# Layer 2 of a four-layer graph kernel: the exact copy of X in two pieces of the rounded four-byte format instead of three bf16 pieces, masks multiplied at full width, every second mask of negative edges made by ScalarE

## The chip, the cores and the metric

The kernel runs on one core of a Trainium2 chip. The metric is the device time of one execution in microseconds (us); lower is better. TensorE (PE in the rows) multiplies, VectorE (DVE), ScalarE (ACT) and GpSimd (POOL) work elementwise, and SyncE (SP) issues most transfers. All wait for one another through semaphores.

## The reference, cut to what matters

`adj` is a 4096 x 4096 float32 matrix with about 1.5% nonzero entries, `x` is 4096 x 64. Four graph layers follow each other, each with a residual and a normalisation. The change is in the second:

```python
node_support = jnp.concatenate([(A_node > 0).astype(h.dtype) @ h, (A_node < 0).astype(h.dtype) @ h], axis=1)
edge_output = gru_cell(node_support, h, w_ih_e, w_hh_e, b_ih_e, b_hh_e)
...
hw = h @ W
h_plus = (node_adj > 0).astype(hw.dtype) @ hw
h_minus = (node_adj < 0).astype(hw.dtype) @ hw
e_plus = jax.nn.leaky_relu(jnp.concatenate([h_plus, h_minus], axis=1) @ a, ALPHA)
...
att = jax.nn.softmax(att, axis=1)
return att * edge_adj @ hw
```

So layer 2 needs four sums over the neighbours of each node: h weighted with the positive and with the negated negative entries of the adjacency matrix (its diagonal taken out), and h summed over the places of the positive and of the negative entries, where the matrix is a 0/1 mask.

## The kernel before

**Layers.** Layer 1 (a polynomial in the matrix, three rounds over it) ends near 501 us of the trace. Layer 2 runs from 529 to 978 us, layer 3 (a product with a decaying weight made from one-byte codes) starts at once behind it, and layer 4 follows. The matrix doesn't fit on the chip, so each layer streams it from memory.

**Layer 2.** The columns are done in `NQ` = 4 quarters (`q`) of 1024. A quarter has `NS` = 8 slots (`s`) of four row blocks of 128, loaded by SyncE with one 2 MB transfer each into one of `RING` = 4 ring slots. A slot is done in two pairs of blocks, so a quarter has `PAIRS` = 16 pairs (`m`), 64 in all. For a pair:

- VectorE extends the chain of neighbour counts that layer 3 needs (L2093, two per pair), makes the masks `more` (L2117, L2122: entry > 0) and `less` (L2118, L2124: entry < 0) in bf16, and then cuts the entries in the ring at zero in place (L2127). That last step needs ScalarE to have read them, and it releases TensorE (`rect_ready`). In four of the sixteen pairs of each quarter VectorE also takes out the diagonal (L2106, L2110, L2113).
- ScalarE makes `negs` (L1453, Relu of the negated entries) and one-byte codes from the chain (L1440), and sends them to memory.
- TensorE multiplies. For each of the two blocks and each half of 512 columns stand there a float32 product of X with the cut entries and one with `negs` (L947, L948), then three products of the bf16 pieces of X with `more` and three with `less` (L953, L955). Every product has 64 output rows; the two of a line number pair take the two halves of the array side by side. The sums lie in banks 0 to 3.

`more`, `less` and `negs` have two places each, so work on pair m may write them as soon as TensorE is done with pair m - 2 (`pair_used`).

**Work between the pairs.** The four queues are written out by hand. While the pairs of quarter q run, the rest of layer 2 for quarter q - 1 and q - 2 is put between them at fixed m: copies of the four sums out of the banks (`copy_sums`, m = 0), `score` (m = 2), score and share arithmetic on VectorE (m = 3 and 5), `weigh_sums` (m = 8), `hidden` on TensorE with `read_hidden` on ScalarE (m = 10 and 11, three banks), the gates (m = 13 to 15 and again at m = 1 and 2 of the next quarter), the normalisation (m = 4, 6, 7) and the pieces of layer 3's operand. In the last quarter ScalarE makes the first two weights of layer 3 (`make_decays`, L1426) at m = 12 and 14. Behind the last pair stand `copy_sums(3)` and `score(3)` ahead of layer 3's first products (`decayed`, L983 and L996).

**Ahead of layer 2** `split` (L1910) and `split_act` (L1228) cut X into its three bf16 pieces, VectorE and ScalarE in turn.

## Time and profile before

| | us |
|---|---|
| median of 3 runs | 1562.92 |
| lowest and highest | 1557.15, 1565.25 |
| the profiled execution | 1558.08 |
| its span, first to last instruction | 1556.3 |
| TensorE busy in the span | 1370.9 (88%) |
| VectorE busy | 1228.1 (79%) |
| ScalarE busy | 922.3 (59%) |
| layer 2, first to last pair | 449 |

The profiled execution is 1.8 us longer than its span and lies 4.8 us below the median. Busy times are sums over instructions, and the products of TensorE overlap in its pipeline: two products that take the two halves of the array count once, and a product starts before the one ahead of it has ended. What a product costs is read from the distance between starts. PEclk is the granted clock of TensorE as a share of its full speed of 2.4 GHz.

### The profile page before, as it was taken

What the parts mean: (1) busy time and instruction counts of PE and PEld (TensorE: products, weight loads), DVE (VectorE), ACT (ScalarE), POOL (GpSimd) and SP (SyncE); (2) the same over time, 40 slices, a digit from 0 to 9 for tenths busy, and PEclk for the clock granted to TensorE, in tenths of its full rate; (3) what the DMA queues carried; (4) which work ended last, traced back from release to release, by engine and by line L of the source; (5) the groups of instructions that cost most, each with busy time, mean ns of one, the idle gap of its engine ahead of it and who ended that gap; (6) DMA issues with size and microseconds to landing.
All of it is one profiled execution on the core that took longest, in us unless ns stands there. A gap on an engine that the chain in (4) does not pass through costs nothing. (4 is left out here: it accounts for less than half of the span.)

```text
span 1556.3 us, 20315 instructions
## 1 busy us (share of the span) xinstructions
PE 1370.9 (88%) x7818; PEld 591.1 (38%) x7818; DVE 1228.1 (79%) x1617; ACT 922.3 (59%) x888; POOL 222.0 (14%) x148
## 2 busy tenths in 40 slices
PE   5999999779977699999999999979977988888970
PEld 1433333223322444444444444534423433333430
DVE  4899866766776877876986977448697898899977
ACT  0000187348743454545555556676788899999964
POOL 1000000000000000000000000134134444444430
PEclk9999999999999699999999999999978999999995
DMA  9999599979999255553543551134723646646600
GB/s 338 409 409 409 232 400 409 413 289 394 409 414 413 109 206 213 179 183 130 183 180 126 183 180 45 55 96 151 240 92 125 199 137 209 209 136 209 215 14 27
DMA packets 135895, 348.92 MB, mean 224 GB/s; under 512 B 7732, under 2 KB 57208, under 8 KB 135544
## 3 DMA queue, kind: packets, MB, share of 16 engines
q1 hardware_dynamic: 119968, 329.27, 57.3%
q10 hardware_dynamic: 15832, 18.36, 3.3%
q8 instruction: 62, 1.02, 0.3%
q14 instruction: 33, 0.27, 0.1%
HBM read 329.78 MB, written 17.83 MB: 223 GB/s over the span
## 5 line engine op out<-in xcount | busy, mean ns | idle before, releaser
L947 PE MATMUL ps<-ring,X 128*64 128x512 f32 x512 | 264.3, 598 | 15.2 <-DVE ring L2127 15.2
L948 PE MATMUL ps<-work,X 128*64 128x512 f32 x512 | 264.3, 598 | 0.0
L1453 ACT ACTIVATE work<-ring 128x2048 f32<-128x2048 f32 x64 | 122.3, 1911 | 156.9 <-PE ps L955 123.4
L953 PE MATMUL ps<-work 128*64 128x512 bf16 x768 | 208.3, 380 | 0.0
L955 PE MATMUL ps<-work 128*64 128x512 bf16 x768 | 208.3, 380 | 0.0
L719 POOL TENSOR_TENSOR ring<-ring,work 128x1024 f32<-128x1024 f32 x72 | 171.1, 2377 | 224.8 <-DVE work L2377 224.8
L816 PE MATMUL ps<-ring,work 128*64 128x512 f32 x672 | 158.1, 615 | 22.8 <-DMA ring<-in_adjT 22.7
L705 POOL TENSOR_SCALAR work<-ring 128x1024 int16<-128x1024 uint8 x24 | 27.7, 1156 | 1008.8 <-DMA ring<-codes 933.1
L953 PEld LDWEIGHTS ps<-work 128*64 128x64 bf16 x768 | 84.8, 110 | 177.9 <-issue 152.4
L1279 ACT ACTIVATE work<-work,code_bias 128x2048 uint8<-128x2048 bf16 (+1 forms) x32 | 62.3, 1947 | 92.0 <-DVE work L1870 82.0
L1214 ACT ACTIVATE turn_in<-ps 128x512 f32<-128x512 f32 x12 | 7.2, 597 | 180.8 <-PE ps L816 180.3
L1834 DVE TENSOR_TENSOR work<-work,ring 128x1024 f32<-128x1024 f32 (+1 forms) x103 | 102.2, 992 | 9.7 <-DMA ring<-in_adjT 8.0
L2127 DVE TENSOR_SCALAR ring<-ring 128x2048 f32<-128x2048 f32 x64 | 78.1, 1220 | 39.5 <-ACT work L1453 39.5
L1079 PE MATMUL ps<-work 64*128 64x512 f32 x288 | 88.1, 691 | 17.6 <-DVE work L2390 16.0
L816 PE MATMUL ps<-ring,X 128*64 128x512 f32 x352 | 85.7, 631 | 17.2 <-DMA ring<-in_adjT 17.2
L816 PE MATMUL ps<-work 128*64 128x512 f32 x352 | 83.3, 618 | 11.1 <-DMA work<-in_adjT 11.1
L816 PEld LDWEIGHTS ps<-ring,work 128*64 128x64 f32 x672 | 45.9, 140 | 122.3 <-issue 86.6
L947 PEld LDWEIGHTS ps<-ring,X 128*64 128x64 f32 x512 | 68.7, 137 | 58.5 <-issue 16.8
L2390 DVE SCALAR_TENSOR_TENSOR work<-ps,work 128x1024 f32<-128x1024 f32 x72 | 87.4, 1214 | 1.1 <-PE ps L1090 1.1
L2122 DVE TENSOR_SCALAR work<-ring 128x2048 bf16<-128x2048 f32 x48 | 58.7, 1224 | 35.7 <-PE ps L955 35.5
L2093 DVE SCALAR_TENSOR_TENSOR stage_words<-ring,stage_words 128x512 bf16<-128x512 f32 x124 | 84.9, 684 | 0.6
L955 PEld LDWEIGHTS ps<-work 128*64 128x64 bf16 x768 | 84.8, 110 | 0.0
(366 smaller groups left out, 2768.1 us busy)
## 6 DMA issues: line engine op xcount, KB each, us to landing
ring<-in_adjT SPq DMA_DIRECT2D x88, 2048.0 KB, 16.0
work<-in_adjT SPq DMA_DIRECT2D x28, 2048.0 KB, 19.7
ring<-in_adjT SPq DMA_DIRECT2D x24, 1024.0 KB, 9.3
ring<-in_adjT SPq DMA_DIRECT2D x48, 512.0 KB, 3.6
ring<-codes SPq DMA_DIRECT2D x32, 512.0 KB, 3.7
ring<-in_adjT SPq DMA_DIRECT2D x64, 256.0 KB, 3.0
codes<-work ACTq DMA_DIRECT2D x32, 256.0 KB, 6.1
codes<-work ACTq DMA_DIRECT2D x64, 128.0 KB, 1.7
```

Source lines behind the costliest of these rows:

```text
L719: nc.gpsimd.tensor_tensor(u.edges, u.edges, u.angle, ALU.mult).then_inc(weighted, 1)
L816: mm = nc.tensor.matmul(ps[i * F:(i + 1) * F, a.banks + h, :], rows_of(a, k), a.room[:, k, cols], start=start, stop=stop)
L947: nc.tensor.matmul(ps[0:F, h, :], rows, ring[:, r, k, cols], start=start, stop=stop)
L948: nc.tensor.matmul(ps[F:P, h, :], rows, negs[:, pair, i, cols], start=start, stop=stop)
L953: nc.tensor.matmul(ps[0:F, 2 + h, :], part, more[:, pair, i, cols], start=start and t == 0, stop=stop and t == 2)
L955: mm = nc.tensor.matmul(ps[F:P, 2 + h, :], part, less[:, pair, i, cols], start=start and t == 0, stop=stop and t == 2)
L1079: mm = nc.tensor.matmul(ps[:, u.banks + h, :].rearrange("p (t c) -> p t c", t=2), UT[h * F:(h + 1) * F, b * P:(b + 1) * P], u.columns(node ...
L1453: nc.scalar.activation(negs[:, pair], ring[:, s % RING, 2 * pair:2 * pair + 2, :], ACT.Relu, scale=-1.0).then_inc(negs_made, 1)
L1834: ins = V.tensor_tensor(sums, sums, edges, ALU.add)
L2093: V.scalar_tensor_tensor(later1[:, (j + 1) % GB, :], edges, 0.0, later1[:, j % GB, :], ALU.not_equal, ALU.add).then_inc(later_made, 1)
L2127: V.tensor_scalar(edges, edges, 0.0, None, ALU.max).then_inc(rect_ready, 1)
L2390: V.scalar_tensor_tensor(u.angle, ps[:, u.banks:u.banks + 2, :].rearrange("p h c -> p (h c)"), 0.5 * DIST_SCALE, u.angle, ALU.max, ALU.add ...
```

## The change

X is cut into two pieces in the type float32r, four bytes wide but rounded: the high piece is X copied to that type by ScalarE, the low piece is X minus the high piece, by VectorE. `more` and `less` become float32r too. The two pieces stand side by side as 128 columns, so one product with a mask gives the sums of both pieces in 128 output rows; the halves are added when the sums are copied out. The mask sums now take banks 2 to 5, four products of 512 columns for each block.

`less` is made by VectorE in even pairs, and in odd pairs by ScalarE as the sign of `negs`. In TensorE's queue the float32 products of both blocks of a pair now come first, then all mask products; those of odd pairs wait for `less_made`.

The four-byte `less` takes the room of one ring slot, so layer 2 has three. `hidden` and `read_hidden` move to m = 11 and 12 and have two banks (three behind the last pair), `supports` moves to m = 10, the first two `make_decays` to m = 14 and 15. Core of the diff:

```diff
-            g, r = s, s % RING
+            g, r = s, slot1(q, s)
...
-                            if start and q:
-                                pe.wait_ge(sums_copied[h], 2 * q)
-                            for t in range(3):
-                                part = parts[:, g * GB + k, t * F:(t + 1) * F]
-                                nc.tensor.matmul(ps[0:F, 2 + h, :], part, more[:, pair, i, cols],
-                                                 start=start and t == 0, stop=stop and t == 2)
-                                mm = nc.tensor.matmul(ps[F:P, 2 + h, :], part, less[:, pair, i, cols],
-                                                      start=start and t == 0, stop=stop and t == 2)
+                    if m % 2:
+                        pe.wait_ge(less_made, (q * PAIRS + m + 1) // 2)
+                    for i in range(2):
+                        k = 2 * pair + i
...
+                        for t, masks in enumerate((more, less)):
+                            if start and q:
+                                pe.wait_ge(sums_copied[0], 3 * q - 1 + t)
+                            for h in range(2):
+                                cols = slice(h * HALF, (h + 1) * HALF)
+                                mm = nc.tensor.matmul(ps[:, 2 + 2 * t + h, :], parts[:, g * GB + k, :],
+                                                      masks[:, pair, i, cols], start=start, stop=stop)
...
+            for n in range(NQ):
...
+                nc.scalar.activation(parts[:, blocks, 0:F], X[:, blocks, :], ACT.Copy)
...
+                    if m % 2:
+                        act.wait_ge(negs_made, q * PAIRS + m + 1)
+                        nc.scalar.activation(less[:, pair], negs[:, pair], ACT.Sign).then_inc(less_made, 1)
...
-                nc.scalar.activation(turn_in[:, HALF:QC], ps[:, 3, :], ACT.Copy).then_inc(sums_copied[1], 1)
+                for t in range(2):
+                    mine, other = slice(t * F, (t + 1) * F), slice((1 - t) * F, (2 - t) * F)
+                    nc.scalar.activation(turn_in[mine, :], ps[other, 2 + 2 * t:4 + 2 * t, :].rearrange(
+                        "p h c -> p (h c)"), ACT.Copy).then_inc(sums_copied[1], 1)
...
+                    V.tensor_tensor(parts[:, blocks, F:2 * F], X[:, blocks, :], parts[:, blocks, 0:F].bitcast(F32),
+                                    ALU.subtract).then_inc(rest_made[0][0], 1)
...
-                V.tensor_copy(turn_in[:, 0:HALF], ps[:, 2, :]).then_inc(sums_copied[0], 1)
+                for t in range(2):
...
+                    dve.wait_ge(sums_copied[1], 3 * n + 2 + t)
+                    V.tensor_tensor(turn_in[mine, :], ps[mine, 2 + 2 * t:4 + 2 * t, :].rearrange("p h c -> p (h c)"),
+                                    turn_in[mine, :], ALU.add).then_inc(sums_copied[0], 1)
```

TensorE's queue at one block and half of a pair in quarter 0, before (the pattern stands four times in a pair):

```order
L947 MATMUL ps<-ring,X 64x512
L948 MATMUL ps<-work,X 64x512
L953 MATMUL ps<-work 64x512
L955 MATMUL ps<-work 64x512
L953 MATMUL ps<-work 64x512
L955 MATMUL ps<-work 64x512
L953 MATMUL ps<-work 64x512
L955 MATMUL ps<-work 64x512
```

The whole of pair 1 of quarter 0 after the change (`more` and `less` are the masks):

```order
L987 MATMUL ps<-ring,X 64x512 [waits rect_ready]
L988 MATMUL ps<-work,X 64x512
L987 MATMUL ps<-ring,X 64x512
L988 MATMUL ps<-work,X 64x512
L987 MATMUL ps<-ring,X 64x512
L988 MATMUL ps<-work,X 64x512
L987 MATMUL ps<-ring,X 64x512
L988 MATMUL ps<-work,X 64x512
L1000 MATMUL ps<-more,parts 128x512 [waits less_made]
L1000 MATMUL ps<-more,parts 128x512
L1000 MATMUL ps<-less,parts 128x512 x2
```

Twelve side-by-side pairs of bf16 products have become eight products of full width (the last row and its like come again for the second block), and the float32 products have moved ahead of them.

ScalarE's queue at the end of the last quarter before, from pair 14 to the copies of the sums. L1453 is `negs`, L1440 the codes, L1426 `make_decays`, L1364 the tanh of the gate, L1412 a piece for layer 3, L1333 and L1334 `copy_sums(3)`:

```order
L1453 ACTIVATE work<-ring 128x2048 [waits pair_used,diag_cut,loaded3]
L1440 ACTIVATE work<-stage_words,code_bias 128x1024 [waits codes_stored0,later_made]
L1443 DMA codes<-work 128x1024 [waits codes_made]
L1426 ACTIVATE ring<-ring,bits_bias 128x3072 [waits pair_used,code_loaded1]
L1453 ACTIVATE work<-ring 128x2048 [waits pair_used,diag_cut,loaded3]
L1440 ACTIVATE work<-stage_words,code_bias 128x1024 [waits codes_stored1,later_made]
L1443 DMA codes<-work 128x1024 [waits codes_made]
L1364 ACTIVATE work<-work 128x1024 [waits new_raw]
L1412 ACTIVATE work<-room_f 128x8x64 [waits rest1_made2]
L1333 ACTIVATE work<-ps 128x512 [waits hid_ready,pair_used]
L1334 ACTIVATE turn_in<-ps 128x512
```

The same place after, from pair 15 (L1494 is `negs`, L1498 the sign, L1480 the codes, L1466 `make_decays`, L1370 and L1373 the copies):

```order
L1494 ACTIVATE work<-ring 128x2048 [waits pair_used,diag_cut,loaded2]
L1498 ACTIVATE less<-work 128x2048 [waits negs_made]
L1480 ACTIVATE work<-stage_words,code_bias 128x1024 [waits codes_stored1,later_made]
L1483 DMA codes<-work 128x1024 [waits codes_made]
L1404 ACTIVATE work<-work 128x1024 [waits new_raw]
L1452 ACTIVATE work<-room_f 128x8x64 [waits rest1_made2]
L1466 ACTIVATE ring<-ring,bits_bias 128x3072 [waits pair_used,code_loaded1]
L1370 ACTIVATE work<-ps 128x512 [waits hid_ready,pair_used]
L1373 ACTIVATE turn_in<-ps 64x1024 x2
```

A sign has been added, and a `make_decays` that stood behind pair 14 now stands directly ahead of the copies.

## Rows read from the trace of the kernel before

**Rows 1.** The page's groups: line engine op out<-in xcount | busy, mean ns | idle before.

```profile
L947 PE MATMUL ps<-ring,X 128*64 128x512 f32 x512 | 264.3, 598 | 15.2 <-DVE ring L2127 15.2
```

**Rows 2.** Windows: length, busy PE, PEld, DVE, ACT, POOL; clock, DMA, GB/s.

```profile
528.80:627.70 98.90, 98.88 (x640) 44.89 (x640) 78.40 (x92) 47.39 (x33) 0.00 (x0) 0.98 0.47 172
627.70:742.80 115.10, 114.67 (x730) 52.98 (x728) 90.45 (x122) 55.89 (x55) 0.00 (x0) 1.00 0.46 165
742.80:859.60 116.80, 116.80 (x748) 54.92 (x746) 98.44 (x137) 62.03 (x66) 0.00 (x0) 1.00 0.45 163
859.60:977.80 118.20, 117.49 (x750) 54.95 (x748) 94.29 (x131) 64.30 (x63) 2.36 (x2) 1.00 0.38 133
977.80:1060.00 82.20, 73.45 (x390) 36.60 (x388) 43.78 (x65) 61.68 (x65) 28.56 (x20) 0.94 0.29 92
...
859.60:873.00 13.40, 13.40 (x92) 5.92 (x90) 13.30 (x17) 7.89 (x7) 0.00 (x0) 1.00 0.49 177
```

**Rows 3.** Timeline of TensorE in pair 15: start us, us, instruction.

```profile
972.54 0.38 PE L953 MATMUL ps<-work 128*64 128x512 bf16 x1
...
973.19 0.59 PE L947 MATMUL ps<-ring,X 128*64 128x512 f32 x1
...
974.05 0.38 PE L953 MATMUL ps<-work 128*64 128x512 bf16 x1
```

**Rows 4.** Timeline of TensorE in layer 3: full width, narrow output, and after idle times.

```profile
988.41 1.90 PE L983 MATMUL ps<-work 128*128 128x512 bf16 x8
990.24 1.05 PE L996 MATMUL ps<-work 128*64 128x512 bf16 x8
...
1030.33 1.89 PE L983 MATMUL ps<-work 128*128 128x512 bf16 x8 [2.60 <-issue]
...
1039.83 3.57 PE L983 MATMUL ps<-work 128*128 128x512 bf16 x8 [4.69 <-issue]
```

**Rows 5.** Weight loads (PEld) in layers 2 and 3: busy us, mean ns | idle.

```profile
L882 PEld LDWEIGHTS ps<-early_w,turn_in 128*128 128x128 f32 x64 | 12.2, 190 | 15.4 <-issue 15.4
```

**Rows 6.** Timeline of VectorE: chain and masks of one pair in quarter 3.

```profile
886.90 0.69 DVE L2093 SCALAR_TENSOR_TENSOR stage_words<-ring,stage_words 128x512 bf16<-128x512 f32 x1
887.51 1.22 DVE L2122 TENSOR_SCALAR work<-ring 128x2048 bf16<-128x2048 f32 x1
...
889.25 1.22 DVE L2124 TENSOR_SCALAR work<-ring 128x2048 bf16<-128x2048 f32 x1
890.39 1.22 DVE L2127 TENSOR_SCALAR ring<-ring 128x2048 f32<-128x2048 f32 x1
891.52 0.16 DVE L1986 TENSOR_SCALAR work<-work 128x8 f32<-128x8 f32 x1
```

**Rows 7.** Timeline of ScalarE: one pair of quarter 3, then the end of layer 2.

```profile
873.02 1.91 ACT L1453 ACTIVATE work<-ring 128x2048 f32<-128x2048 f32 x1 [3.07 <-PE ps L955]
874.84 1.13 ACT L1440 ACTIVATE work<-stage_words,code_bias 128x1024 uint8<-128x1024 bf16 x1
...
964.53 2.86 ACT L1426 ACTIVATE ring<-ring,bits_bias 128x3072 int16<-128x3072 uint8 x1 [0.46 <-ACT work L1440]
...
978.91 1.02 ACT L1341 ACTIVATE work<-ps 64x1024 f32<-64x1024 f32 x1
```

**Rows 8.** Timeline of VectorE and TensorE at quarter boundaries.

```profile
859.82 0.68 DVE L1943 COPY work<-ps 128x512 f32<-128x512 f32 x1
...
979.32 2.18 PE L859 MATMUL ps<-w_score,turn_in 128*128 128x2 f32 x16 [0.45 <-DVE turn_in L1944]
```

**Rows 9.** Timeline at the start of layer 2.

```profile
515.49 1.29 DVE L1910 TENSOR_TENSOR Y<-X,work 128x512 f32<-128x512 f32 x2 [0.47 <-ACT work L1228]
...
521.47 0.91 DVE L1916 MEMSET work<- 1x1024 f32 x1 [0.27 <-issue]
...
528.82 1.09 PE L947 MATMUL ps<-ring,X 128*64 128x512 f32 x1 [14.03 <-DVE ring L2127]
```

**Rows 10.** Transfers issued from 528 to 980 us: KB each, median us to landing.

```profile
ring<-in_adjT SPq DMA_DIRECT2D x28, 2048.0 KB, 8.6
```

155 lines of the change are left out of this document (86 added, 69 removed).

## The prediction, made before the changed kernel ran

> **What bounds the kernel now.** I read the page's groups first, then layer 2 in windows of one quarter, then the timelines of TensorE, VectorE and ScalarE. In the whole of layer 2 the two float32 products wait 15.2 us for anything, and nearly all of it once, at the start [rows 1, 9]. By quarters TensorE is busy 98.9 of 98.9, 114.7 of 115.1, 116.8 of 116.8 and 117.5 of 118.2 us [rows 2]. So TensorE sets the pace, and what is taken off its queue counts, until something else is late. The reader should see who that is: VectorE is busy 78, 90, 98 and 94 us in the same windows, and 13.30 of 13.40 us at the start of the last quarter [rows 2]. ScalarE has 47 to 64 us. So the cover over VectorE is thin in quarters 2 and 3.
>
> Of one block and half, the three bf16 steps run from 972.54 to 973.19 (0.65 us, 0.214 a step) and the float32 step from 973.19 to 974.05 (0.86 us, four times 0.214) [rows 3]. Together 1.5 us, four times in a pair: 6.0 us, of which masks 2.57. 64 pairs are 383 us of layer 2's 449; the rest is work between the pairs and a slow first pair.
>
> **TensorE's mask products.** Gone are 12 steps a pair, added are 8 of full width in float32r. No row shows that type. The lower bound is the bf16 step: 0.214 side by side [rows 3], 0.229 at full width (988.41 to 990.24, eight products) [rows 4]. The upper bound is a float32 product of the same columns, 0.86. I take the lower: the float32 product costs exactly four bf16 steps, as if each operand went through in two parts, and here a mask is 0 or 1 and each piece of X is rounded to the format, so nothing is left for further parts. The Trainium skill, page "FP8 and Floating Point Precision", section "TensorE Precision Notes", says that true float32 takes four passes and that a reduced form reads four bytes and cuts them; by that the eight products take 1.7 us a pair, and the four steps in our row agree with its first half, while no run yet shows the second.
>
> Masks then take 8 x 0.214 = 1.71 to 8 x 0.229 = 1.83 us a pair instead of 2.57: 0.86 to 0.74 off, **55 to 47 us over 64 pairs** if nothing else is late. At the upper bound it is 6.9 us a pair, 4.3 more, 275 us lost.
>
> The weights are now 128 columns of four bytes. Such a load takes 190 ns [rows 5], still under the 214 of the product it lies beside, so it is hidden; with no overlap a step would be 0.40. The Trainium skill, page "TensorE: Matmul & The Clock Gate", section "Weight-path perf modes — Fast Weight Load (FWL) and DoubleRow", speaks against the change here: the fast load serves 128 weights that are not float32. By it the new weights might lose that, and the sum would move only if the load outlasted the product.
>
> **VectorE.** Its steps in a pair start 0.61, 1.14, 0.60, 1.14 and 1.13 us apart: chain, `more`, chain, `less`, cut; 4.62 in all [rows 6]. A four-byte output costs what a two-byte one does (1.22 for L2127 and for L2122 [rows 6]), so `more` stays. Odd pairs lose `less`: 3.48. That is 32 x 1.14 = 36 us less. Added are, per quarter, two adds of 1024 columns out of the banks (1.22 each, like other operations of two operands) for one copy of 0.6: 1.9 more. Bound from above: a rounded output at half the rate, 1.1 us more for each of the 96 masks that VectorE still makes.
>
> **ScalarE.** 32 signs of 2048 columns, by the Relu of that size 1.91 each [rows 7]: 61 us more, in a queue that now idles 3.1 us ahead of a Relu [rows 7]. An odd pair is 1.8 + 1.9 + 1.6 (codes with their transfer) = 5.3 us, an even one 3.4, against TensorE's 5.1. The sign is needed 3.4 us into the pair, behind the float32 products, so it hides. Queued behind it are the codes, and at the end of a quarter the tanh of the gate, for which VectorE waits.
>
> **What is late next.** I stepped the three queues pair by pair through the four quarters, each instruction starting at the latest of the one ahead and what it waits for, with the distances above and TensorE two mask places ahead at most. Done for the kernel before, this gives 448 us for layer 2 (the trace: 449). With 0.214 a mask step it gives 416, with 0.229 420. By quarters: 13 to 14 off in quarter 0, where only masks are made; 10 in quarter 1; 3 each in quarters 2 and 3. There some 12 us of new waits eat nearly all of the 13.7: before pairs 0 and 1 (3.3 and 1.2), 4, 6 and 8 (1.3, 2.3, up to 1.9), and pair 15 of the last (2.2).
>
> The largest, worked out, from the end of pair 15 of quarter 2 as zero: ScalarE ends its Relu at -8.4, sign -6.4, codes -4.8, tanh -3.8. VectorE's update of the gate (2.4) ends at -1.3, then 0.35 to open the chain and 4.6 for pair 0: +3.7, copy +4.3. TensorE has 1.1 us of transposes and stands 3.2. Before, the same path ended with the copy at about +0.8, while the transposes ran: the trace has that copy at 859.82, 0.2 after the last pair began to drain [rows 8]. Two banks in place of three for `hidden` cost 0.5 to 1.2 once a quarter. **Layer 2: -30 us**, the mean of -32 and -28.
>
> **The start.** `split` takes its turns from 515.49 and VectorE goes on at 521.47 [rows 9]; four copies and four subtractions of 0.69 end at 518.3. VectorE is what TensorE waits for there (14.03 us): **-3 us**.
>
> **Behind the last pair.** `make_decays` (2.86 [rows 7]) now stands directly ahead of the copies. Relu, sign and codes of pair 15 end at -2.8, tanh and piece -1.3, `make_decays` +1.6. Then a copy to +2.1, the two of 64x1024 (1.02 each [rows 7]) to +4.1, VectorE's last add to +5.5. `score` starts at 979.32 now, 1.5 us behind the pairs [rows 8], and then at 5.7; layer 3's first products and the gates stand behind it, so **+4 us**. 4.7 us of idle was followed by products at 3.57 for eight instead of 1.89, 2.6 us was not [rows 4]: 0.5 more.
>
> **The ring.** Three slots instead of four: a load is issued when its slot is free, about 14 us before VectorE wants it; it lands in 8.6 [rows 10]. Nothing. The first transfer of codes waits two pairs longer, but its user has moved two pairs too. Nothing. The new waits in `row_spread` and `turn_rows` end long before: nothing.
>
> **Sum**, against the profiled execution: 1558.1 - 3 - 30 + 4.5 = 1529.6. It lies 4.8 below the median of the runs; I put half of that back: **1532 us**.
>
> **The rivals.**
> 1. *VectorE and ScalarE keep up* (the new waits are mostly absent): 55 - 8 in layer 2 gives 1558 - 3 - 47 + 4 = 1512. For it: one pair of slack that my stepping may place badly. Against it: 13.30 of 13.40 busy.
> 2. *The clock*: TensorE's new waits at quarter starts (3.3 us) lie between the idle of 2.6 that left the clock at 2.4 GHz and the one of 4.7 that took it to 1.2 [rows 4]. Three such falls, 2.5 us each: 1540. I keep this inside the forecast's range.
> 3. *VectorE writes the rounded type at half rate*: 2.28 for a mask, so an even pair takes it 6.9 us and an odd one 4.6. The stepping gives 482 for layer 2: 1558 - 3 + 34 + 4.5 = 1593.
> 4. *Slower: the rounded product is not one step.* At two steps (0.43), or with the 190 ns load in the open (0.40), masks take 3.4 a pair; it decides from 0.32, where 8 x 0.32 is today's 2.57. The stepping gives 497 for layer 2: 1558 - 3 + 49 + 2 = 1606. At four steps 715: 1824. For it: no row shows the type. Against it: the argument from 0/1 masks.
>
> **How the numbers follow.** Forecast with the clock's falls 0.76, rival 1 0.10, rival 3 0.05, rival 4 0.09. The range leaves out rivals 3 and 4 and what lies below rival 1: 1510 to 1556. Faster than 1562.9 by over 0.5% (about what a measurement of this kernel can tell from no change) is below 1555: rival 1 and nearly all of the forecast, 0.82. The forecast's upper end, where some of the waits are double, gives 0.04 for the same. Slower: 0.14.
>
> **What would show it.** Mask products start 0.21 to 0.23 apart (0.43 or 0.86: rival 4). `more` takes 1.22 (2.3: rival 3). Quarters of about 85, 105, 113 and 115 us (about 85, 102, 103 and 105: rival 1). TensorE waits for VectorE's cut or its copies some 12 us in each of quarters 2 and 3. VectorE is busy over 90 of 113 us. `score(3)` starts 5 to 6 us behind the last pair. Layer 4's stretch stays at 496 us. It would be wrong if the waits of quarters 2 and 3 had another place, or if layer 4 moved.

## The result and the profile after

| | before | after |
|---|---|---|
| median us (4 runs each) | 1562.42 | 1546.10 |
| lowest and highest | 1557.15, 1565.25 | 1539.45, 1547.75 |
| profiled execution (span) | 1558.08 (1556.3) | 1546.3 (1544.5) |

The ratio is 0.9906, 95% interval [0.988, 0.9932]: 0.9% faster. The forecast was 1532 (-30 us); -16 us came. The direction and the range held the result, the size did not: layer 2 gave half of what was forecast, and the stretch behind it took more.

In the two profiled executions layer 2 starts 4.5 us earlier, its 449.0 us become 432.8, the stretch from the last pair to the first product of the fold (L1005 before, L1050 after) grows from 82.2 to 88.9, and the rest takes 498.4 instead of 496.3. Together that is the difference of the spans, -11.8. The rest, which the change doesn't touch, was forecast to stay at 496; of its 2.1 us more, 1.6 are time in which TensorE's granted clock was at half. The windows after, cut at the quarters and at the fold, answer [rows 2] (length, busy PE, PEld, DVE, ACT, POOL; clock, DMA, GB/s):

```profile
524.30:616.40 92.10, 92.05 (x384) 40.62 (x385) 70.19 (x84) 62.69 (x41) 0.00 (x0) 0.98 0.53 184
616.40:725.90 109.50, 106.67 (x474) 53.12 (x473) 81.25 (x112) 72.25 (x64) 0.00 (x0) 1.00 0.49 172
725.90:841.30 115.40, 110.59 (x491) 55.75 (x490) 92.01 (x130) 78.76 (x76) 0.00 (x0) 0.99 0.47 164
841.30:957.10 115.80, 110.73 (x493) 56.00 (x492) 90.80 (x127) 80.59 (x73) 2.69 (x2) 0.99 0.43 150
957.10:1046.00 88.90, 74.75 (x382) 37.72 (x387) 45.74 (x67) 64.18 (x67) 28.06 (x20) 0.92 0.28 92
```

Forecast were quarters of about 85, 105, 113 and 115; they are 92.1, 109.5, 115.4 and 115.8. The miss is largest in quarter 0, where TensorE is busy all the time: so its work is dearer than the sum said. In quarters 2 and 3 it is busy 110.6 of 115.4 and 110.7 of 115.8, so it waits 4.8 and 5.1 us there, not 12.

One pair of quarter 0 on TensorE (start us, us; the side-by-side partner L988 of each L987 is left out, and the trace has two rows for each float32 product), which answers [rows 3]:

```profile
560.31 0.64 PE L987 MATMUL ps<-ring,X 128*64 128x512 f32 x1
560.79 0.59 PE L987 MATMUL ps<-ring,X 128*64 128x512 f32 x1
561.22 0.59 PE L987 MATMUL ps<-ring,X 128*64 128x512 f32 x1
...
563.37 0.59 PE L987 MATMUL ps<-ring,X 128*64 128x512 f32 x1
563.89 0.73 PE L1000 MATMUL ps<-more,parts 128*128 128x512 f32 x2
564.47 0.62 PE L1000 MATMUL ps<-less,parts 128*128 128x512 f32 x2
564.93 0.62 PE L1000 MATMUL ps<-more,parts 128*128 128x512 f32 x2
565.38 0.61 PE L1000 MATMUL ps<-less,parts 128*128 128x512 f32 x2
565.93 0.64 PE L987 MATMUL ps<-ring,X 128*64 128x512 f32 x1
```

Read the distances of starts. Between the rows of float32 products: 0.428, so 0.86 for a product. Between two full-width mask products: 0.455 to 0.46, so 0.228 each: one step, as forecast. But at the places where the width changes there is more: 563.37 to 563.89 is 0.52 (0.10 over the float32 step); 563.89 to 564.47 is 0.58 for two products (0.12 over); 565.38 to 565.93 is 0.55 (0.095 over); 560.31 to 560.79 is 0.48 (0.05 over). That is 0.37 a pair, and the pair takes 3.42 + 8 x 0.228 + 0.37 = **5.62 us** and not 5.14 to 5.25.

The start of quarter 2. First ScalarE and VectorE (columns as before; in brackets the idle time ahead and its releaser), then TensorE:

```profile
716.82 1.91 ACT L1498 ACTIVATE less<-work 128x2048 fp32r<-128x2048 f32 x1
...
720.17 1.06 ACT L1404 ACTIVATE work<-work 128x1024 f32<-128x1024 f32 x1 [0.40 <-ACT work L1480]
...
721.26 1.23 DVE L2060 TENSOR_TENSOR work<-X,work 128x1024 f32<-128x1024 f32 x1 [2.78 <-ACT work L1404]
...
723.78 0.35 DVE L2127 TENSOR_SCALAR stage_words<-work,not_first 128x512 bf16<-128x512 bf16 x1
...
727.72 1.22 DVE L2173 TENSOR_SCALAR ring<-ring 128x2048 f32<-128x2048 f32 x1
...
728.86 0.69 DVE L1981 COPY work<-ps 128x512 f32<-128x512 f32 x1
```

```profile
729.69 0.61 PE L987 MATMUL ps<-ring,X 128*64 128x512 f32 x1 [2.79 <-DVE work L1981]
730.14 0.92 PE L987 MATMUL ps<-ring,X 128*64 128x512 f32 x1
730.85 1.06 PE L987 MATMUL ps<-ring,X 128*64 128x512 f32 x1
731.71 1.06 PE L987 MATMUL ps<-ring,X 128*64 128x512 f32 x1
732.56 1.06 PE L987 MATMUL ps<-ring,X 128*64 128x512 f32 x1
733.41 0.73 PE L987 MATMUL ps<-ring,X 128*64 128x512 f32 x1
733.98 0.59 PE L987 MATMUL ps<-ring,X 128*64 128x512 f32 x1
```

Sign, codes, tanh, the gate's update, chain, pair 0's cut, copy, product: the path of the prediction, step for step, ending in a wait of 2.79 us (3.3 were worked out). Behind it the products start 0.85 us apart instead of 0.43 for a while, and TensorE loses 1.7 us. A window there shows the granted clock at 0.50, which is 1.2 GHz:

```profile
730.70:733.50 2.80, 2.80 (x10) 1.00 (x8) 2.77 (x3) 2.77 (x2) 0.00 (x0) 0.50 0.99 400
```
The start of quarter 3 (845.13) reads the same, wait and loss: another 2.79 us, and another 1.7 us of half clock.

Behind the last pair (its drain starts at 957.12), which answers [rows 8]:

```profile
957.81 0.57 ACT L1370 ACTIVATE work<-ps 128x512 f32<-128x512 f32 x1
958.41 2.06 ACT L1373 ACTIVATE turn_in<-ps 64x1024 f32<-64x1024 f32 x2
959.46 2.47 DVE L1985 TENSOR_TENSOR turn_in<-ps,turn_in 64x1024 f32<-64x1024 f32 x2 [1.39 <-ACT turn_in L1373]
961.99 3.25 PE L895 MATMUL ps<-w_score,turn_in 128*128 128x2 f32 x16 [3.83 <-DVE turn_in L1985]
```

`score(3)` starts 4.9 us behind, where it was 1.5.

### The profile page after: what moved, and what is told of

It is laid out like the page before. It is cut to its first block and busy times, and to the rows that moved or that the text cites. A ratio compares the mean times of both kernels' runs of the same rounds, so it can differ in the third digit from the quotient of the medians.

```text
span 1544.5 us, 18239 instructions
## 1 busy us (share of the span) xinstructions
PE 1341.8 (87%) x6769; PEld 590.3 (38%) x6794; DVE 1200.4 (78%) x1585; ACT 985.3 (64%) x916; POOL 221.8 (14%) x148
## 5 line engine op out<-in xcount | busy, mean ns | idle before, releaser
L987 PE MATMUL ps<-ring,X 128*64 128x512 f32 x512 | 239.0, 610 | 22.4 <-DVE ring L2173 16.8
L988 PE MATMUL ps<-work,X 128*64 128x512 f32 x512 | 239.0, 611 | 0.0
L1494 ACT ACTIVATE work<-ring 128x2048 f32<-128x2048 f32 x64 | 122.3, 1911 | 92.6 <-PE ps L1000 59.2
L987 PEld LDWEIGHTS ps<-ring,X 128*64 128x64 f32 x512 | 66.2, 139 | 154.1 <-issue 139.3
L2173 DVE TENSOR_SCALAR ring<-ring 128x2048 f32<-128x2048 f32 x64 | 78.4, 1224 | 50.8 <-ACT work L1494 50.3
L851 PE MATMUL ps<-ring,X 128*64 128x512 f32 x352 | 85.3, 629 | 18.2 <-DMA ring<-in_adjT 18.2
L851 PEld LDWEIGHTS ps<-ring,work 128*64 128x64 f32 x672 | 45.9, 140 | 122.0 <-issue 86.3
L1000 PE MATMUL ps<-more,parts 128*128 128x512 f32 x256 | 86.7, 420 | 0.0
L1000 PE MATMUL ps<-less,parts 128*128 128x512 f32 x256 | 79.7, 392 | 0.0
L2167 DVE TENSOR_SCALAR more<-ring 128x2048 fp32r<-128x2048 f32 x48 | 58.8, 1224 | 25.3 <-PE ps L1000 25.3
L1914 DVE SCALAR_TENSOR_TENSOR work<-ring,work 128x512 bf16<-128x512 f32 x85 | 58.5, 688 | 24.0 <-DMA ring<-in_adjT 19.7
L1644 ACT ACTIVATE work<-work 128x1024 f32<-128x1024 f32 x72 | 75.4, 1048 | 1.9 <-DVE work L2436 0.5
```

Source lines behind the costliest of these rows:

```text
L851: mm = nc.tensor.matmul(ps[i * F:(i + 1) * F, a.banks + h, :], rows_of(a, k), a.room[:, k, cols], start=start, stop=stop)
L987: nc.tensor.matmul(ps[0:F, h, :], rows, ring[:, r, k, cols], start=start, stop=stop)
L988: nc.tensor.matmul(ps[F:P, h, :], rows, negs[:, pair, i, cols], start=start, stop=stop)
L1000: mm = nc.tensor.matmul(ps[:, 2 + 2 * t + h, :], parts[:, g * GB + k, :], masks[:, pair, i, cols], start=start, stop=stop)
L1494: nc.scalar.activation(negs[:, pair], ring[:, r, 2 * pair:2 * pair + 2, :], ACT.Relu, scale=-1.0).then_inc(negs_made, 1)
L1644: nc.scalar.activation(v.angle, v.angle, ACT.Ln, scale=2.0 / DIST_SCALE).then_inc(angle_made, 1)
```

## The experiments

All times are medians; ratios are against the kernel before, run on the same chip in turn with the kernel (0.9906 is the changed kernel's). Layer 2 by quarters, from the traces, in us; *clock* is what quarters 1 to 3 lost with the granted clock at half (the length times what the clock lacked); *score* is its distance from the last pair:

| kernel | q0 | q1 | q2 | q3 | sum | clock | score | ratio |
|---|---|---|---|---|---|---|---|---|
| before | 98.9 | 115.1 | 116.8 | 118.1 | 449.0 | 0 | 1.5 | 1 |
| after | 92.1 | 109.4 | 115.4 | 115.8 | 432.8 | 3.4 | 4.9 | 0.9906 |
| e1 alternate | 89.2 | 108.1 | 115.4 | 117.6 | 430.3 | 5.1 | 4.3 | 0.9906 |
| e2 interleave | 97.4 | 113.4 | 119.9 | 120.3 | 451.1 | 3.4 | 4.4 | 1.0015 |
| e3 bf16, wide | 89.5 | 108.9 | 113.1 | 114.3 | 425.8 | 5.1 | 5.1 | 0.9850 |
| e4 decay late | 92.3 | 109.4 | 115.4 | 115.3 | 432.5 | 1.7 | 4.4 | 0.9892 |
| e5 no sign | 91.8 | 113.2 | 115.6 | 116.9 | 437.5 | 1.7 | 4.4 | 0.9951 |
| e6 `less` once | 92.6 | 109.0 | 110.8 | 112.5 | 424.8 | 0 | 4.4 | 0.9830 |
| e7 plain copies | 92.6 | 107.8 | 113.7 | 114.0 | 428.1 | 0 | 2.9 | 0.9846 |
| e8 e1 and e4 together | 89.7 | 108.1 | 115.4 | 117.7 | 431.0 | 3.4 | 4.3 | 0.9890 |
| e9 last sign | 92.1 | 109.4 | 112.6 | 113.9 | 428.0 | 0 | 4.4 | 0.9883 |
| e10 before, sign | 99.1 | 114.5 | 121.3 | 119.6 | 454.4 | 1.7 | 1.5 | 1.0050 |
| e11 alternate, even signs | 89.7 | 112.4 | 112.0 | 113.7 | 427.9 | 1.7 | 4.3 | 0.9874 |
| e12 cut first | 98.0 | 116.1 | 124.4 | 122.0 | 460.6 | 8.5 | 4.4 | 1.0046 |
| e13 wait moved | 89.2 | 110.2 | 112.0 | 115.3 | 426.8 | 1.7 | 4.3 | 0.9894 |
| e14 early copies | 89.1 | 111.8 | 112.0 | 113.7 | 426.6 | 1.7 | 2.4 | 0.9862 |
| e15 masks ahead | 90.0 | 109.1 | 110.9 | 112.3 | 422.3 | 0 | 2.7 | 0.9801 |

Sums are to be compared less the clock's column. A fall costs 1.7 us (one in e12, and one behind layer 2 in e10, lasted longer and cost more), and whether it comes changes between executions of the same instructions: up to pair 15 of quarter 3 the queues of e4 are those of the changed kernel, TensorE waits as long at both quarter starts, and the clock fell behind both waits in the changed kernel, in e4 behind the first alone. Here is the second of e4, with no fall behind it:

```profile
846.05 0.61 PE L987 MATMUL ps<-ring,X 128*64 128x512 f32 x1 [2.78 <-DVE work L1982]
```

### What a pair costs on TensorE: e1, e2, e3

Theory: each change between side-by-side 64-row products and full-width ones costs a fixed time. e1 halves the changes, e2 doubles them, e3 keeps them and takes the four-byte type away.

e1, odd pairs take the masks first (`counted` is the eight mask products, `exact` the float32 ones), so that one pair ends as the next begins:

```diff
+                    if m % 2:
+                        counted()
+                        mm = exact()
+                    else:
+                        exact()
+                        mm = counted()
```

> Odd pairs of layer 2 multiply their masks first and the float32 products second, so that the masks of an even pair and of the odd pair behind it stand in one row: one change between halves-of-the-array products and full-width products per pair instead of two. Theory A (each such change costs TensorE about 0.19 us): a pair of quarter 0 goes from 5.62 us to about 5.43, layer 2 is 8 to 12 us shorter, the time some 8 us below the changed kernel (about 1538). Theory B (the rounded products themselves cost more than 0.214 us, and changes nothing): a pair stays at 5.62 us and the time at 1546.

Measured: 1542.44, ratio 0.9906 [0.9883, 0.993]. Two pairs take 10.85 us, 5.43 each: 2 x (3.42 + 1.83) + 0.37.

e2, float32 and mask products of each block in turn, four changes a pair (the wait for ScalarE's sign moves ahead of the pair with them):

```diff
+                    if m % 2:
+                        pe.wait_ge(less_made, (q * PAIRS + m + 1) // 2)
                     for i in range(2):
                         k = 2 * pair + i
...
-                    for i in range(2):
-                        k = 2 * pair + i
-                        start = m == 0 and i == 0
-                        stop = m == PAIRS - 1 and i == 1
                         for t, masks in enumerate((more, less)):
```

> Float32 and mask products of one block stand together, as block 0, masks 0, block 1, masks 1: four changes of width per pair instead of two. Theory A: a pair goes from 5.62 us to about 6.0, and the time rises by 20 to 24 us over the changed kernel (1566 to 1570), above the kernel before. Theory B: a pair stays at 5.62 us and the time within 3 us of 1546, since the number and kinds of products are the same.

Measured: 1561.07, ratio 1.0015 [0.9993, 1.0037]. A pair takes 5.98 to 6.0 us (5.99 by the same sum with 2 x 0.37): 18 us more in layer 2 (20 to 24 in time were expected, 15 came), and the whole gain of the change is gone.

e3, pieces and masks in bf16 at full width (the products are right in number and shape, but the two pieces no longer hold all bits of X):

```diff
-            less = under.enter_context(nc.sbuf_tensor("less", [P, 2, 2, QC], F32R))
+            less = under.enter_context(nc.sbuf_tensor("less", [P, 2, 2, QC], BF16))
...
-            parts = under.enter_context(nc.sbuf_tensor("parts", [P, NB, 2 * F], F32R))
+            parts = under.enter_context(nc.sbuf_tensor("parts", [P, NB, 2 * F], BF16))
```

> The two pieces of X and both masks in bf16 instead of the rounded four-byte type, all else as in the changed kernel; the sums then lack the part of X below the second bf16 piece. Theory A in the form that the width alone costs: a pair stays near 5.6 us and the time near 1546. Theory C (the four-byte type costs: its weight load of 128 columns stands in the open at each change, or its products are slower): a pair falls to 5.2 to 5.3 us, the rounded step of 0.228 to 0.214, and the time to about 1530.

Measured: 1534.86, ratio 0.985 [0.9827, 0.9872]. Its pair on TensorE (the rows begin at its mask products and end at those of the next pair):

```profile
560.93 0.60 PE L1000 MATMUL ps<-more,parts 128*128 128x512 bf16 x2
561.38 0.59 PE L1000 MATMUL ps<-less,parts 128*128 128x512 bf16 x2
561.81 0.59 PE L1000 MATMUL ps<-more,parts 128*128 128x512 bf16 x2
562.24 0.59 PE L1000 MATMUL ps<-less,parts 128*128 128x512 bf16 x2
562.76 0.64 PE L987 MATMUL ps<-ring,X 128*64 128x512 f32 x1
...
566.35 0.60 PE L1000 MATMUL ps<-more,parts 128*128 128x512 bf16 x2
```

5.42 us from 560.93 to 566.35, a product every 0.216. So of the 0.48 us by which the pair missed the forecast's lower figure (5.14), 0.25 come from the two changes of width whatever the type, 0.12 from the first rounded product (0.58 for two, where e3 has 0.45), and 0.11 from steps of 0.228 instead of 0.214. The theory of the change of width stands; the type adds some 0.2, nearly as much again, so neither figure expected for e3 (5.6, or 5.2 to 5.3) was met.

Where the width changes, the type changes too, from float32 to a mask's type, and no run separates the two. The kernel before does: its side-by-side products change from float32 to bf16 and back eight times a pair, and three bf16 steps take 0.65 and the float32 one 0.86 there, with nothing on top [rows 3]. So the type's change alone costs nothing, and the width's is what is paid for.

But e1 also says something else: 0.19 us off each pair would be 12 us, and layer 2 got only 2.5 shorter, quarter 2 not at all and quarter 3 longer. One more fall of the clock, behind a wait of 2.5 us for pair 15's sign, is 1.7 of what is missing, and longer waits are 2.5. And where full-width work of another step stands behind an odd pair's float32 products, the change of width comes back: in quarter 1 two pairs alone take 10.87 us instead of 11.24, two with `hidden` among them 23.31 instead of 23.35. Less the falls, layer 2 is 4.2 us shorter. TensorE alone no longer sets the time there.

### What waits in quarters 2 and 3: e5, e6, e9

e5, VectorE makes all masks, no sign on ScalarE:

```diff
-                        if m % 2 == 0:
-                            V.tensor_scalar(less[:, pair], edges, 0.0, None, ALU.is_lt)
+                        V.tensor_scalar(less[:, pair], edges, 0.0, None, ALU.is_lt)
```

> VectorE makes every mask of negative edges, ScalarE makes none by sign; all else as in the changed kernel. Theory: after the masks have shrunk, VectorE and TensorE share the limit in quarters 2 and 3, so 32 masks of 1.14 us (36 us) on VectorE show in part. Stepping the three queues with the pair of 5.62 us that the trace has (it gives 433 for layer 2 of the changed kernel, as measured) gives 440: quarters 0 and 1 within 1 us of 92 and 109, quarters 2 and 3 about 3 us longer each, with waits of the mask products for VectorE. Time about 7 us above the changed kernel. Rival (the sign is what makes it faster): 36 us of VectorE come back nearly whole, +20 us or more. Rival (VectorE has room, sign is worth nothing): within 2 us.

Measured: 1553.12, ratio 0.9951 [0.993, 0.9972]; layer 2 437.5 (440 by the stepping, 432.8 with the sign). The sum is near, the places are not: quarter 1 lost 3.8 us, of which 1.7 are a fall of the clock, quarter 2 only 0.2, where a fall of 1.7 is missing. Less the falls, the 32 masks cost layer 2 6.4 us (435.8 against 429.4). There TensorE's first product reads

```profile
733.83 0.61 PE L987 MATMUL ps<-ring,X 128*64 128x512 f32 x1 [0.84 <-DVE work L1976]
```

a wait of 0.84 instead of 2.79, and no fall of the clock behind it. So the sign has a price too: that of pair 15 stands ahead of the tanh, and without it the wait is 1.9 us shorter.

e6, `less` is made in quarter 0 only and left as it is:

```diff
-                        if m % 2 == 0:
+                        if m % 2 == 0 and q == 0:
                             V.tensor_scalar(less[:, pair], edges, 0.0, None, ALU.is_lt)
...
-                    if m % 2:
+                    if m % 2 and q == 0:
                         act.wait_ge(negs_made, q * PAIRS + m + 1)
```

> The masks of negative edges are made in quarter 0 alone and used as they stand in quarters 1 to 3 (those are left out of the computation); TensorE does all its products. Theory (TensorE's pair of 5.62 us is most of what is left, and VectorE's and ScalarE's queues cost about 9 us of waits in quarters 2 and 3): layer 2 about 424 instead of 433, quarters 2 and 3 about 111 each, quarter 1 at 109. Time about 8 us below the changed kernel. Rival (the waits eat most, as the prediction had it: 12 us in each of quarters 2 and 3): 20 us or more below.

Measured: 1535.39, ratio 0.983 [0.9802, 0.9858]; layer 2 424.8. With 8 to 10 us of VectorE's and 15 of ScalarE's work gone in each of quarters 2 and 3, they give 4.6 and 3.3 us, 1.7 of each being the fall that doesn't come, and TensorE's 109 us of work are the floor. The rival (12 us of waits in each) falls.

e9, VectorE makes `less` of pair 15, and ScalarE's signs end with pair 13:

```diff
+        SIGNS = (1, 3, 5, 7, 9, 11, 13)
...
-                    if m % 2:
+                    if m in SIGNS:
                         act.wait_ge(negs_made, q * PAIRS + m + 1)
```

> As the changed kernel, but VectorE makes the mask of negative edges of pair 15 in each quarter, so ScalarE's sign (1.91 us) no longer stands ahead of the tanh for which VectorE's gate waits. Theory (the 2.79 us waits at the starts of quarters 2 and 3 come from that sign, and the first of them brings the clock's fall, 1.7 us): the waits shrink to about 0.9 as in the kernel with every such mask on VectorE (0.84), no fall behind them, quarters 2 and 3 each 2 to 4 us shorter (115.4 to about 112, 115.8 to about 113.5), time 4 to 6 us below the changed kernel, ratio about 0.987. Rival (VectorE's total work sets these quarters, one mask more costs 1.1 us each): quarters at 115 to 117, ratio 0.990 or above.

Measured: 1542.26, ratio 0.9883 [0.986, 0.9905]. The two quarter starts wait 0.84 and 0.85 us, the products behind follow at 0.43, and quarters 2 and 3 are 2.8 and 1.9 us shorter: 428.0 against 432.8, the lower end of what was expected. Of these 4.8 us, 3.4 are the two falls, and e4 and e7 show that a fall can stay away with the wait as it was; the waits themselves are 2 us shorter, and only that is surely the sign's. In time that is 3.6 us by the two ratios, whose intervals overlap, so the verdict rests on the traces.

### Behind the last pair: e4, e7

e4, `make_decays(1)` behind the copies instead of ahead:

```diff
-                    if q == NQ - 1 and m in (14, 15):
-                        make_decays(m - 14)
+                    if q == NQ - 1 and m == 14:
+                        make_decays(0)
...
             copy_h(3)
+            make_decays(1)
```

> The second make_decays of ScalarE moves from ahead of the last copies of sums to behind them. Theory D (this move is what delays score(3) from 1.5 to 4.9 us behind the last pair): score(3) starts 1.5 to 2.5 us sooner, and the time falls by 2 to 5 us, more than the shift itself if TensorE's clock stays up. Rival: the two copies of 64x1024 and the two adds are the delay by themselves, and layer 3 waits for the weight instead; score(3) moves by under 1 us or layer 3's first products take the wait over, time unchanged.

Measured: 1542.83, ratio 0.9892 [0.9871, 0.9914]; `score(3)` 4.4 us behind the last pair instead of 4.9. The prediction had blamed this step for most of the delay; it is 0.5 us of it.

e7, the wide banks copied as in the kernel before, one copy of 512 columns on each engine and no adds:

```diff
-                for t in range(2):
-                    mine, other = slice(t * F, (t + 1) * F), slice((1 - t) * F, (2 - t) * F)
-                    nc.scalar.activation(turn_in[mine, :], ps[other, 2 + 2 * t:4 + 2 * t, :].rearrange(
-                        "p h c -> p (h c)"), ACT.Copy).then_inc(sums_copied[1], 1)
+                nc.scalar.activation(turn_in[:, HALF:QC], ps[:, 3, :], ACT.Copy).then_inc(sums_copied[1], 2)
```

> The sums are copied as in the kernel before, one copy of 512 columns on each engine for the wide banks and no adds: this leaves out the sums of the second piece and of the other half. Theory (the 4.9 us from the last pair to score are ScalarE's two copies of 64x1024 and VectorE's two adds, one behind the other): score(3) starts 1.5 to 2 us behind the last pair, and the stretch from the last pair to the fold falls from 89 to 84 or 85 us; quarters 1 to 3 gain up to 1 us each at their start. Time 4 to 7 us below the changed kernel. Rival (something else holds score, such as the queue ahead of the copies): score still 4 us or more behind, time within 2 us.

Measured: 1535.98, ratio 0.9846 [0.9821, 0.9872]. `score(3)` starts 2.9 us behind and the stretch to the fold is 87.9 instead of 88.9: two copies and two adds in a chain are what holds it, yet 2 us there bring 1 at the fold, where e7 has one fall of the clock more than the changed kernel (8.5 us lost in the stretch against 6.8). The quarters fell by 1.6 to 1.8 each, and not for the reason expected. In quarter 1 the wait of 1.4 us at pair 1 is gone. In quarters 2 and 3 the waits are all as they were, but for one thing:

```profile
845.71 0.61 PE L987 MATMUL ps<-ring,X 128*64 128x512 f32 x1 [2.79 <-DVE work L1979]
...
846.16 0.59 PE L987 MATMUL ps<-ring,X 128*64 128x512 f32 x1
...
846.59 0.59 PE L987 MATMUL ps<-ring,X 128*64 128x512 f32 x1
...
847.02 0.59 PE L987 MATMUL ps<-ring,X 128*64 128x512 f32 x1
```

The same wait of 2.79 us as in the changed kernel, and the clock stays at 2.4 GHz. The same 1.7 us that the fall had cost there are missing here. So the fall is not decided by the length of this wait alone; by what else stays open.

Over the 17 traces, layer 2 behind its first product has 35 waits of TensorE over 2 us. A fall comes behind 14 of the 26 between 2 and 3 us, behind 8 of the 9 longer ones, and behind 1 of the 56 between 1 and 2 us. The shortest of the 22 is 2.07 us (e2).

### The sign by itself, and the order on VectorE: e10, e12

e10, the kernel before with nothing of the change but ScalarE's sign in odd pairs; TensorE waits for it ahead of the pair:

```diff
+                    if m % 2:
+                        pe.wait_ge(less_made, (q * PAIRS + m + 1) // 2)
...
+                    if m % 2:
+                        act.wait_ge(negs_made, q * PAIRS + m + 1)
+                        nc.scalar.activation(less[:, pair], negs[:, pair], ACT.Sign).then_inc(less_made, 1)
...
-                        V.tensor_scalar(less[:, pair], edges, 0.0, None, ALU.is_lt)
+                        if m % 2 == 0:
+                            V.tensor_scalar(less[:, pair], edges, 0.0, None, ALU.is_lt)
```

> The kernel before, with ScalarE's sign for the odd pairs' masks of negative edges and nothing else of the change. Theory (TensorE alone bounds layer 2 of the kernel before, so a freer VectorE is worth nothing there): within 2 us of the kernel before, ratio 0.999 to 1.002; the longer ScalarE queue ahead of the gate could cost 1 us at quarter starts. Rival (VectorE was half of the bound before, too): 3 us or more faster.

Measured: 1567.45, ratio 1.005 [1.0033, 1.0067]. Slower, past both expectations: TensorE had no use for a freer VectorE, and now waits 2.1 us for the copy at the start of quarter 2 and runs at half clock behind, and 1.9 us at the start of quarter 3. The row of the first:

```profile
744.46 1.03 PE L950 MATMUL ps<-ring,X 128*64 128x512 f32 x1 [2.14 <-DVE work L1949]
```

Layer 2 is 5.4 us longer by it. The stretch to the fold is longer too, 92.1 us instead of 82.2, and for another reason: behind a wait of 1.79 us for VectorE ahead of L895 the clock stays at half for 13.7 us there, which costs 6.8, and what the sign has to do with that isn't shown.

This half of the change thus costs 0.5% alone and saves about 0.5% beside the other half (e5 against after, whose intervals just touch). e12 cuts the edges first and makes `more` and `less` behind the cut:

```diff
                     V.tensor_scalar(edges, edges, 0.0, None, ALU.max).then_inc(rect_ready, 1)
+                    dve.wait_ge(rect_ready, q * PAIRS + m + 1)
+                    made = V.tensor_scalar(more[:, pair], edges, 0.0, None, ALU.is_gt)
+                    if m not in SIGNS:
+                        made = V.tensor_scalar(less[:, pair], negs[:, pair], 0.0, None, ALU.is_gt)
+                    made.then_inc(masks_made, 1)
```

> VectorE cuts the edges first and makes the masks behind (more from the cut edges, less from ScalarE's negated ones), copies the first bank between them, and pair 15 has no sign on ScalarE. The float32 products, first in TensorE's queue, need only the cut. Theory (the waits of quarters 2 and 3 and the one at the start are latency, VectorE's queue being full but ahead of TensorE by less than a pair): the cut comes 1.2 to 2.4 us sooner in each pair, the wait at the start of layer 2 falls from 10.8 to about 8.5, the waits at quarter starts vanish, layer 2 about 421 to 424, ratio about 0.983. Rival (VectorE's sum of work is what holds quarters 2 and 3, and an order within the pair moves nothing): layer 2 above 428, ratio 0.988 or above.

Measured: 1567.52, ratio 1.0046 [1.0029, 1.0063]. Layer 2 takes 460.6, 33 more than e9: 22 of it are TensorE's waits, 32.6 us against 10.9, and 10 are the clock's falls behind them, of which e9 has none behind its first wait. VectorE's groups in the last quarter (count, busy us, mean ns, idle ahead and its releaser), first of after, then of e12:

```profile
L2173 DVE TENSOR_SCALAR ring<-ring 128x2048 f32<-128x2048 f32 x16 | 19.6, 1225 | 16.0 <-ACT work L1494 15.8
```

```profile
L2171 DVE TENSOR_SCALAR ring<-ring 128x2048 f32<-128x2048 f32 x16 | 19.6, 1227 | 20.9 <-ACT work L1497 20.6
```

The cut waits for ScalarE's Relu, 15.8 us in the last quarter even in the changed kernel. The masks don't wait for it; made ahead of the cut they fill that time, behind it they come on top. So VectorE, 91 us busy in 116, is not full in quarter 3, and neither theory of this run was right. The reading that fits is the loop: TensorE's last product on pair m - 2, Relu, cut, TensorE; no run takes it apart.

### The waits at their places: e11, e13, e14, e15

e11 is e1 with the signs in pairs 2, 4 ... 14, whose mask products come last:

```diff
+        SIGNS = (2, 4, 6, 8, 10, 12, 14)
```

> Products alternate (odd pairs masks first, half the changes of width) and ScalarE's signs serve pairs 2, 4 ... 14, where the float32 products come first and hide them; none stands ahead of the tanh at a quarter's end. Theory (the alternating order lost its 5 us of layer 2 to waits for the sign and at the quarter starts): the waits for ScalarE's mask (3.9 us) vanish, quarters about 89, 107, 111, 113, so layer 2 about 421 instead of 430, time 8 to 11 us below the changed kernel, ratio about 0.985. Rival (VectorE's total work is the bound once TensorE's pair is 5.43): quarters 2 and 3 stay at 115 or more, ratio 0.990.

Measured: 1540.11, ratio 0.9874 [0.9851, 0.9896]. Quarters 2 and 3 fell as thought, quarter 1 rose from e1's 108.1 to 112.4: its waits grew by 2.4 us, since the one for the sign stood ahead of the pair's float32 products, and a fall of 1.7 came behind the longest. e13 moves it (the lines are against e11):

```diff
-                    if m in SIGNS:
-                        pe.wait_ge(less_made, q * len(SIGNS) + SIGNS.index(m) + 1)
                     if m % 2:
                         counted()
                         mm = exact()
                     else:
                         exact()
+                        if m in SIGNS:
+                            pe.wait_ge(less_made, q * len(SIGNS) + SIGNS.index(m) + 1)
                         mm = counted()
```

> As the kernel with alternating products and ScalarE's signs in pairs 2, 4 ... 14, but TensorE waits for the sign where its mask is first read, behind the pair's float32 products, and not ahead of them. Theory (the 3.9 us that TensorE waits there for the sign is my misplaced wait, and with it gone layer 2 is limited by the loop from TensorE's last product over the Relu to the cut): the wait for the sign vanishes, quarter 1 from 112.4 to 109 or less, layer 2 about 424 instead of 427.9, ratio about 0.985. Rival (whatever TensorE gains comes back as waits for VectorE's cut): layer 2 at 427 or above, ratio 0.987.

Measured: 1543.02, ratio 0.9894 [0.9866, 0.9922]. The 3.9 us for the sign are gone, the waits for the cut ahead of mask products rose from 6.9 to 8.8 us and one more of 2.0 came: 1.1 us off layer 2, with one fall of the clock in each of the two. At 426.8 the rival (427) fits, the theory (424) doesn't; the time tells nothing, since the intervals overlap. e14 sends the last sums off behind pair 15's masks, which in this order stand ahead of its float32 products (against e13):

```diff
+                        if q == NQ - 1 and m == PAIRS - 1:
+                            mm.then_inc(last_masks, 1)
                         mm = exact()
```

> The kernel of the run before, and at the end of the last quarter the counted sums are copied and added behind pair 15's mask products, which there stand 3.4 us ahead of its last float32 product; the weighted sums' copies and make_decays(1) come behind. Theory (score(3) is late by the chain of two copies of 64x1024 and two adds, 3.3 us, with nothing else behind it): score(3) starts 2.3 to 3 us behind the last pair instead of 4.4, as in the kernel that leaves out the adds (2.9), and the stretch from the last pair to the fold falls by 1 to 2 us; ratio about 0.984. Rival (the stretch behind is limited by the decays and their clock, so score's place is worth nothing): the fold at the same distance within 0.5 us, time unchanged against the run before.

Measured: 1538.31, ratio 0.9862 [0.9841, 0.9884]. `score(3)` starts 2.4 us behind, and the fold 86.7 instead of 88.4. The 1.7 us are as much as the one fall that this stretch has fewer than e13's; whether the earlier `score` keeps it away isn't shown, and the intervals of the two times overlap. e15 lets the mask products of odd pairs wait for the masks and not for the cut behind them (against e14):

```diff
-                    pe.wait_ge(rect_ready, q * PAIRS + m + 1)
+                    if m % 2:
+                        pe.wait_ge(masks_made, q * PAIRS // 2 + (m + 1) // 2)
+                    else:
+                        pe.wait_ge(rect_ready, q * PAIRS + m + 1)
```

> The kernel of the run before (alternating products, signs in even pairs, early copies), and TensorE's mask products of odd pairs, which stand first there, wait for the masks alone and no longer for the cut behind them. Theory (the 8.8 us of waits ahead of those products, six times, are for a cut of 1.14 us that they don't read): each falls by 1.1 to 1.2 us, 6 or 7 us in all, and what part of it stays depends on the float32 products behind, which need the cut 1.9 us later: layer 2 about 421 instead of 426.6, ratio 0.982 to 0.984. Rival (TensorE's gains come back as waits at the next pair, since the loop from its last product over the Relu to the masks stays as long): layer 2 at 425 or above, ratio 0.986.

Measured: **1530.91, ratio 0.9801 [0.9771, 0.983]**, the fastest of all and 1% below the changed kernel; layer 2 422.3. Of the 4.3 us below e14, 1.7 are the fall that e14 has in quarter 1; of the 10.5 below the changed kernel, 3.4 are falls, so the order and the places of waits gave 7.1. In the two profiled executions the stretch behind the fold, which none of this touches, adds to the difference: 491.3 us against 498.4, nearly all of it clock. Its windows by quarter:

```profile
530.20:620.20 90.00, 90.00 (x384) 41.79 (x384) 71.16 (x85) 60.83 (x40) 0.00 (x0) 0.97 0.55 189
620.20:729.30 109.10, 105.00 (x475) 53.34 (x473) 84.05 (x115) 70.99 (x63) 0.00 (x0) 1.00 0.50 174
729.30:840.20 110.90, 107.92 (x493) 55.29 (x491) 92.94 (x131) 77.51 (x74) 0.00 (x0) 1.00 0.49 171
840.20:952.50 112.30, 108.35 (x494) 55.39 (x492) 90.77 (x127) 78.75 (x72) 2.63 (x2) 1.00 0.44 154
```

TensorE waits 3.0 and 3.9 us in quarters 2 and 3. One more run, e8, put e1 and e4 together:

> The alternating order of the products (odd pairs with the masks first) and the last make_decays behind the copies, together. Each alone gave within 1 us of the changed kernel's time (1542.4 and 1542.8 against 1546.1 in another set of runs). Theory (the time is no longer set by TensorE alone in quarters 2 and 3, and make_decays hides nothing): 0 to 3 us below the changed kernel, last stretch within 1 us of 89. Rival (the two gains add up to a visible one): 5 us or more below.

It gave 1543.76, ratio 0.989 [0.9863, 0.9917]; layer 2 took 431.0. The time can't be told from that of either alone, as the theory had it.

## Why the prediction was off

**The mask step: the term that failed.** "Masks then take 8 x 0.214 = 1.71 to 8 x 0.229 = 1.83 us a pair instead of 2.57". They take 2.20: eight steps of 0.228 and 0.37 for two changes between products that share the array and products that fill it. So a pair became shorter by 0.38 us and not by 0.74 to 0.86, about 24 us over 64 pairs instead of 47 to 55. The claim under it held: the rounded product is one step (rival 4 had 0.43 and more). What was missed is that the change also alters the *order of kinds*: before, all products of a pair share the array. A row of the trace of before could have told it. In layer 3, where bf16 products of 128 and of 64 rows alternate, they start 0.31 to 0.34 us apart, against 0.23 unmixed [rows 4]:

```profile
1051.15 0.38 PE L988 MATMUL ps<-stage_words,work 128*128 128x512 bf16 x1
1051.46 0.40 PE L989 MATMUL ps<-stage_words,work 128*64 128x512 bf16 x1
1051.80 0.39 PE L988 MATMUL ps<-stage_words,work 128*128 128x512 bf16 x1
1052.12 0.40 PE L989 MATMUL ps<-stage_words,work 128*64 128x512 bf16 x1
```

The 190 ns weight load was called hidden [rows 5]; in a row of mask products nothing of it shows, but the first rounded product behind the float32 ones costs 0.12 us that e3 doesn't have. The Trainium skill, page "FP8 and Floating Point Precision", section "TensorE Precision Notes", gives true float32 four passes and knows a reduced form that reads four bytes and cuts them; the step of 0.228 for the rounded type, against four times 0.214 for float32, agrees. The Trainium skill's page "TensorE: Matmul & The Clock Gate" (section "Weight-path perf modes — Fast Weight Load (FWL) and DoubleRow") gives the fast load to 128 weights that aren't FP32, and doesn't say where the rounded type stands; the 0.12 us a pair may be its loss, but the runs show the price and not its cause.

**The new waits, 12 us in each of quarters 2 and 3: too many.** They were 4.8 and 5.1. With the true pair of 5.62 the stepping gives 433 for layer 2, and the trace has 432.8; but 3.4 of these are falls of the clock, which the stepping doesn't know, so it is some 4 us over, as it is for e5 (440, where the trace less its fall has 435.8). The longer pair had eaten the waits, so half of the first error was cancelled by the second, which is luck: 64 x 0.38 to 0.48 is 24 to 31 us, and layer 2 missed by 14 (432.8 against 416 to 420).

**The start, -3: right.** `split` ends at 517.00 instead of 521.47 and TensorE waits 10.81 instead of 14.03; the other 1.2 us of the 4.5 came ahead of `split`.

**Behind the last pair, +4.5: it is +6.7, with the wrong culprit.** `make_decays` costs 0.5 (e4). The chain of copies and adds costs 2 (score from 4.9 to 2.9 in e7, from 4.3 to 2.4 in e14). `score` is 3.4 us later by its start. Of the other 3.4, two are the clock: `score` takes 3.25 us behind its wait of 3.83, instead of 2.18 [rows 8], and behind 2.60 us of idle seven products take 2.58, where before eight took 1.89 behind the same idle [rows 4]; a later fall is 1.2 cheaper. The last 1.3 are a wait for VectorE ahead of L934, 1.52 us where the kernel before has 0.18 (L894 at 1027.08), of which the prediction has no word:

```profile
1012.69 0.66 PE L934 MATMUL ps<-ident,Y 128*128 128x128 f32 x4 [1.52 <-DVE Y L2104]
1015.94 2.58 PE L1028 MATMUL ps<-work 128*128 128x512 bf16 x7 [2.60 <-issue]
```

**Rivals.** The clock's fall (rival 2) came, at the starts of quarters 2 and 3, 1.7 us each; 2.5 were reckoned. Its two rows, 2.6 us that left the clock up and 4.7 that took it down [rows 4], were too few to go by: falls came in layer 2 behind 2.07 us. VectorE at half rate (rival 3) is refuted, 1224 ns for `more` in the page's group:

```profile
L2167 DVE TENSOR_SCALAR more<-ring 128x2048 fp32r<-128x2048 f32 x48 | 58.8, 1224 | 25.3 <-PE ps L1000 25.3
```

Rival 1 (the others keep up) is half true: there are 9.9 us of waits in quarters 2 and 3 instead of some 24, and 3.4 of clock behind them. ScalarE's sign, called hidden, is hidden but for pair 15's. The ring of three slots cost nothing: TensorE waits for no load in layer 2.

## What to carry to other kernels

Cost a TensorE edit by the neighbours as well as by the step: look in the trace for a row where two kinds of product alternate before multiplying a step by a count. Put each wait ahead of the first instruction that reads what it guards, and each short task of a helping engine where nobody waits behind it: in e15 such moves, with the alternating order, took 7 us more off layer 2, the clock's falls left out. Read the granted clock of both traces before explaining a difference of 2 us: several of the steps above are a fall of 1.7 us that came or stayed away. And don't take an engine that is 80% busy for full: ask in which order it waits, and for whom.
